# Five matrix places in the convolution, row scatters without pacing waits, and the second layer's output bias added by VectorE

## The reference, cut to what matters

```python
# layer 1, convolution: v, x1, x2 are three projections of the normalised input
y = v
for i, kern in enumerate((k0, k1)):
    y = fft_conv(y, kern) * x[i + 1]          # 128 channels, 128 taps, causal
x = residual + y @ W_out + b_out
# layer 1, experts: 8 experts, each token goes to 2 of them
h = gelu(einsum("td,ndh->tnh", xt, w1) + b1)
out_all = einsum("tnh,nhd->tnd", h, w2) + b2   # b2 is the output bias of the change
out = (take_along_axis(out_all, top_i) * top_w).sum(axis=1)
```

## Time and profile before

| | us |
|---|---|
| median of 3 runs | 1197.08 |
| lowest and highest of them | 1195.99, 1204.09 |
| the profiled execution, its own time | 1201.37 |
| span of its trace, first to last instruction | 1199.5 |
| convolution: first to last gate | 746.4 to 876.0 |
| experts of layer 1: first to last evacuation | 888.5 to 1158.6 |

### The profile page before, as it was taken

How to read it: one execution, slowest core, us unless ns; L and a number is a source line. 1 busy time by engine, 2 the same in 40 slices (tenths; PEclk the granted TensorE clock), 3 DMA queues, 4 the chain that set the end, 5 groups by cost and what they waited for, 6 DMA issues and landing times. The chain is left out here.

```text
span 1199.5 us, 21003 instructions
## 1 busy us (share of the span) xinstructions
PE 1015.5 (85%) x7025; PEld 881.2 (73%) x7025; DVE 946.0 (79%) x1636; ACT 543.9 (45%) x1511; POOL 788.7 (66%) x685
## 2 busy tenths in 40 slices
PE   5636777798999999999834699988989999999994
PEld 4612333367888888888724599988889999999994
DVE  7777999999999999999999874111268887778848
ACT  1301111157888787888714583000045555555541
POOL 4147766658888888888878357777636665656640
PEclk9868777899999999999956989999999999999998
DMA  9923233325565565665372033999912222442239
GB/s 290 377 83 133 91 127 126 116 69 157 172 189 168 173 175 171 178 185 173 93 293 106 36 102 102 322 292 378 347 51 66 70 68 65 124 148 68 66 116 343
DMA packets 119884, 192.20 MB, mean 160 GB/s; under 512 B 16426, under 2 KB 88190, under 8 KB 117730
## 3 DMA queue, kind: packets, MB, share of 16 engines
q1 hardware_dynamic: 100896, 154.30, 40.4%
q0 software_dynamic: 17408, 35.32, 8.0%
q10 hardware_dynamic: 1474, 1.24, 0.4%
HBM read 123.77 MB, written 67.03 MB: 159 GB/s over the span
## 5 line engine op out<-in xcount | busy, mean ns | idle before, releaser
L560 POOL DMA_INDIRECT y_tok<-FF,yidx x278 | 306.2, 1102 | 164.6 <-DVE FF L1440 103.3
L552 POOL DMA_INDIRECT sorted_x<-XN,idx x256 | 247.7, 967 | 99.1 <-issue 79.1
L887 PE MATMUL ps<-FF 128*128 128x128 f32 x1680 | 204.7, 275 | 0.0
L887 PEld LDWEIGHTS ps<-FF 128*128 128x128 f32 x1680 | 195.8, 192 | 12.0 <-issue 9.0
L344 POOL TENSOR_TENSOR BG<-TPB 128x2048 f32<-128x2048 f32 (+1 forms) x42 | 160.9, 3858 | 14.1 <-DVE BG L1268 13.7
L918 PE MATMUL ps<-BG,cst 128*128 128x512 f32 x176 | 106.8, 775 | 47.9 <-DVE BG L1242 47.9
L1277 DVE TENSOR_TENSOR BG<-ps,TPB 128x1024 f32<-128x1024 f32 x128 | 147.3, 1212 | 0.0
L1286 DVE TENSOR_REDUCE BG<-BG 128x256 f32<-128x4096 f32 x32 | 139.4, 4358 | 0.0
L869 PE MATMUL ps<-FF 128*128 128x256 f32 x568 | 134.5, 380 | 0.0
L918 PEld LDWEIGHTS ps<-BG,cst 128*128 128x128 f32 x176 | 43.2, 252 | 106.3 <-issue 55.3
L631 ACT ACTIVATE FF<-ps,FF 128x256 f32<-128x256 f32 x284 | 114.9, 479 | 7.3 <-PE ps L869 7.0
(11 more groups left out here) (229 smaller groups left out, 2106.2 us busy)
## 6 DMA issues: line engine op xcount, KB each, us to landing
FF<-in_moe SPq DMA_DIRECT2D x71, 514.0 KB
TPB<-in_kpad SPq DMA_DIRECT2D x22, 1024.0 KB, 8.0
sorted_x<-TPB SPq DMA_DIRECT2D x36, 520.0 KB, 4.3
FF<-sorted_x SPq DMA_DIRECT2D x135, 130.0 KB, 2.2
BG<-y_tok SPq DMA_DIRECT2D x12, 1024.0 KB, 9.9
FF<-in_kpad SPq DMA_DIRECT2D x10, 1024.0 KB, 8.0
y_tok<-FF,yidx POOLq DMA_INDIRECT x278
xt_d<-BG SPq DMA_DIRECT2D x16, 256.0 KB, 4.0
```

Source lines behind the costliest of these rows:

```text
L552: pool.indirect_dma_start(sorted_x[layer], bass.IndirectOffsetOnAxis(ap=idx[:, k, j:j + 1], axis=0), XN[:, j, :], None).then_inc(s_sc[part ...
L560: pool.indirect_dma_start(y_d[layer], bass.IndirectOffsetOnAxis(ap=yidx[:, G % 4, r:r + 1], axis=0), ys[:, G % 4, r * D:(r + 1) * D], None ...
L887: t = pe.matmul(psY[:, r * P:(r + 1) * P], hT[:, G % 2, m, r * P:(r + 1) * P], (wc[:, G % 4, :] if layer == 0 else block_weights(f, r))[:, ...
```

## The change

Four things are changed at once.
- The convolution has five matrix places instead of three. The two new ones lie in `FF[:, 0:4096]`, where the first weight places `wb` are; so the first two `tile_weights`, which stood between the last convolution steps, now follow the convolution.
- `beside_tensor_engine` leaves out its waits in layer 1.
- The output bias is no longer copied per block nor written by a matmul. A resident float32 set `box`, spread to all partitions by one DMA, is read by VectorE: `expert_evac` loads the block's expert number, adds `box[e]` to `psY` into a scratch tile `yb`, waits for that with the new semaphore `s_yb`, and scales from `yb` to `ys`.
- The loops of layer 1 are written in another order: PE does hidden(f), rows_X(f+1), expert_out(f-1); VectorE does rows_T(f+1), expert_evac(f-1), tile_weights(f+3). Four of the 16 copies of the convolution's result stand ahead of the loop, the other 12 in every second tile from the first.

```diff
+TPS = 5
-                    wait(sp, s_cmm, N - 2)
+                    wait(sp, s_cmm, N - TPS + 1)
-                    if cv == 1 and 2 <= n < 2 + E:
-                        expert_weights(n - 2)
+                    if cv == 1 and 5 <= n < 5 + E:
+                        expert_weights(n - 5)
...
-                elif n < 34:
-                    if n >= 6 and n % 4 == 2:
-                        pool.wait_ge(s_pps, min(14 + n // 2, NT // 2))
-                elif n >= 40 and n % 6 == 4:
-                    pool.wait_ge(s_cmm, min((n - 40) // 3 + 1, 2 * D // 8))
...
-                pe.matmul(psY[:, 0:FT].rearrange("p (r d) -> p r d", r=FR), ones3[:, :],
-                          bo[:, G % 4, None, :].to_broadcast([P, FR, D]) if layer == 0 else block_biases(f),
-                          start=True, stop=False)
+                if layer == 0:
+                    pe.matmul(psY[:, 0:FT].rearrange("p (r d) -> p r d", r=FR), ones3[:, :],
+                              bo[:, G % 4, None, :].to_broadcast([P, FR, D]), start=True, stop=False)
...
             for f in range(NF1):
+                hidden(1, f)
                 if f + 1 < NF1:
                     rows_X(1, f + 1)
-                hidden(1, f)
...
-                    t = dve.tensor_copy(block_biases(f)[:, r:r + 1, :], box[:, ds(e, 1), :])
...
                 for r in range(FR):
-                    t = dve.tensor_scalar(ys[:, G % 4, r * D:(r + 1) * D], psY[:, r * D:(r + 1) * D],
+                    e = dve.value_load(eid[0:1, 2 * f + r:2 * f + r + 1], min_val=0, max_val=E - 1)
+                    t = dve.tensor_tensor(yb[:, r * D:(r + 1) * D].rearrange("p (a n) -> p a n", a=1),
+                                          psY[:, r * D:(r + 1) * D].rearrange("p (a n) -> p a n", a=1),
+                                          box[:, ds(e, 1), :], ALU.add)
+                t.then_inc(s_yb, 1)
+                dve.wait_ge(s_yb, f + 1)
+                for r in range(FR):
+                    t = dve.tensor_scalar(ys[:, G % 4, r * D:(r + 1) * D], yb[:, r * D:(r + 1) * D],
                                           xs[:, G % 4, r, D + 1:D + 2], None, ALU.mult)
                 t.then_inc(s_yev, 1)
...
+            gather_outputs(0)
+            gather_outputs(1)
+            gather_outputs(2)
+            gather_outputs(3)
+            rows_T(0)
             tile_weights(2)
-            gather_outputs(0)
-            rows_T(0)
-            rows_T(1)
             for f in range(NF1):
+                if f + 1 < NF1:
+                    rows_T(f + 1)
                 if f > 0:
                     expert_evac(f - 1)
-                if f + 2 < NF1:
-                    rows_T(f + 2)
```

More of the change, by code:

```diff
@@ L102, in mixed_layers @@
         w1s = sb("w1s", [P, W_END])
+        bix = sb("bix", [P, E, MK])
         w3s = sb("w3s", [LAT, LAT + 2 * D + P - LAT + 1])
@@ L171, in mixed_layers @@
         wb = [a[:, i * 1028:(i + 1) * 1028] for a in (FF, TPB) for i in range(4)]
-        box = xg[:, 0, :].bitcast(bf16).rearrange("p (e n) -> p e n", e=E)
-        bix = xg[:, 1, 0:E * MK].rearrange("p (e m) -> p e m", e=E)
-        bot = xg[:, 1, 2 * E * MK:2 * E * MK + 256].bitcast(bf16).rearrange("p (s n) -> p s n", s=4)
+        box = xg.rearrange("p s (e n) -> p (s e) n", n=D)
+        yb = bo[:, :, :].rearrange("p s n -> p (s n)").bitcast(fp32)
         wc = FF[:, 0:4112].rearrange("p (s n) -> p s n", s=4)
@@ L194, in mixed_layers @@
         patr = pat.rearrange("p (r d) -> p r d", r=FILL)
-        tp = [a.rearrange("p (c n) -> p c n", c=8) for a in (TPB[:, 0:2048], TPB[:, 2048:4096], FF[:, 5664:7712])]
+        tp = [a.rearrange("p (c n) -> p c n", c=8) for a in (TPB[:, 0:2048], TPB[:, 2048:4096], FF[:, 5664:7712],
+                                                    FF[:, 0:2048], FF[:, 2048:4096])]
         ps = [ctx.enter_context(nc.psum_tensor(f"ps{i}", [P, 512], fp32)) for i in range(8)]
@@ L281, in mixed_layers @@
         s_gev = sem("second_gate_ready")
-        s_tp = [sem(f"toeplitz_loaded{i}") for i in range(3)]
+        s_tp = [sem(f"toeplitz_loaded{i}") for i in range(TPS)]
         s_cmm = sem("conv_psum")
@@ L888, in expert_out @@
                                       (wc[:, G % 4, :] if layer == 0 else block_weights(f, r))[:, HID + m * D:HID + (m + 1) * D],
-                                      start=False, stop=(r == FR - 1 and m == MK - 1))
+                                      start=(layer == 1 and m == 0),
+                                      stop=(m == MK - 1 and (layer == 1 or r == FR - 1)))
                 t.then_inc(s_Y, 1)
@@ L1019, in convolution @@
                         c0 = k * NT + NT // 2
-                        pe.matmul(bank[:, k * NT:k * NT + n0], tp[N % 3][:, k, diag:diag + P], V[:, col:col + n0],
+                        pe.matmul(bank[:, k * NT:k * NT + n0], tp[N % TPS][:, k, diag:diag + P], V[:, col:col + n0],
                                   start=True, stop=False)
-                        t = pe.matmul(bank[:, c0:c0 + n1], tp[N % 3][:, k, P - diag:2 * P - diag], V[:, col:col + n1],
+                        t = pe.matmul(bank[:, c0:c0 + n1], tp[N % TPS][:, k, P - diag:2 * P - diag], V[:, col:col + n1],
                                       start=False, stop=True)
@@ L1394, in _ @@
             dve.wait_ge(s_resst, 16 * 8)
-            dve.memset(xg[:, :, :], 0.0).then_inc(s_bz, 1)
             for g in range(NG):
@@ L1420, in _ @@
                 conv_gate(1, n, X2)
-                if n == 12:
-                    dve.wait_ge(s_bx, 32)
-                    dve.wait_ge(s_wx, 16 * E)
-                if n in (12, 14):
-                    tile_weights((n - 12) // 2)
             dve.wait_ge(s_cev, 32)
+            dve.wait_ge(s_bx, 32)
+            dve.wait_ge(s_wx, 16 * E)
+            tile_weights(0)
+            tile_weights(1)
             def rows_T(f):
@@ L1459, in _ @@
                     tile_weights(f + 3)
-                if 0 < f < 2 * NG and f % 2 == 0:
-                    gather_outputs(f // 2)
+                if f % 2 == 0 and f // 2 + 4 < NG:
+                    gather_outputs(f // 2 + 4)
                 if f >= NF1 - 18 and f % 2 == 0 and f < NF1 - 2:
```

14 lines of the change are left out of this document (5 added, 9 removed).

## The result

The kernel after takes 1246.9 us (median of 4 runs, 1243.48 to 1248.06) against 1197.78 (4 runs, 1195.99 to 1204.09): the ratio is 1.041 with a 95% interval of 1.038 to 1.043. Its profiled execution took 1247.55 us, span 1245.7, so it stands 0.7 above the median where that of before (1201.37) stands 3.6 above, or 4.3 above the median of three runs that the prediction had.

What follows compares the result with a forecast made beforehand. PE was taken to bound the experts before, the psY ring after. Terms -9 + 40.8 + 13 + 1.8 = +46.6 us on the profiled 1201.4 gave 1248; less 4.3 for the median, 1244 rounded; range 1212 to 1264.

Steps and rivals of the forecast that it cites:

- front, to the first index copy: Convolution and start of the experts: five places and unpaced scatters start the experts 9 us earlier (bounds 0 and 12).
- 67 plain steps: Experts of layer 1: 67 tile steps at 4.63 us each, 310.2 us against 269.4, 40.8 us more.
- extra copies: Expert tiles with a convolution-result copy (12) or residual add (8) come late: 13 us together, bounds 0 and 17.
- from the last index copy to the end: Last evacuation, on the path to the end, grows from 0.68 to 2.44 us: 1.8 us more.
- The ring with two exposed loads: Experts: output and evacuation alternate through one bank psY; two number loads lengthen this to 4.63 us, above PE's 3.79.
- A waiting instruction holds up the loads behind it: VectorE's evacuation: number loads behind the index copy that waits for psY cannot start until it does; 0.76 us each.
- The rival that they run ahead of it: Evacuation: both loads finish while the index copy waits for psY, PE stays the bound, 1177 us; chance 0.08.
- The price of a load: VectorE's evacuation: a number load delays the next instruction needing it by some 0.76 us, bounds 0.73 and 0.80.
- The new order costs nothing by itself: Expert loop: PE's hidden products ahead of the transposes add nothing at 4.63 us per tile, with 0.25 to spare.
- The bias matmul's 0.11: Experts: without the bias matmul PE loses 0.11 us per tile, its own work becoming 3.79 us.
- The rival of one hidden load: Evacuation: first load hides under the transposed-rows copy, VectorE's list binds at 4.15, 278 us; total 1216 or 1207; chance 0.07.
- The clock: PE in the experts: granted clock stays 1.00; the rival that it falls gave 1280 us, chance 0.06.

Runs made afterwards that it cites:

- e1: Kernel after, with the bias adds reading fixed rows of the bias set, so the evacuation's two number loads are gone; 1201.44 us, ratio 1.0025.
- e7: Kernel after, with expert numbers kept in registers from the weight copies instead of loaded again, and the expert loop in the old order; 1190.11 us, ratio 0.994.

## Why the prediction was right, and where not

The median was forecast at 1244 us, in a range of 1212 to 1264, and came to 1246.9; against the median of before that is 49.1 us more. Against the span of before (+46.2 measured, +46.6 predicted) the four terms are:

| term | predicted | measured |
|---|---|---|
| front, to the first index copy | -9 | -4.9 |
| 67 plain steps | +40.8 | 67 x 4.51 - 269.4 = +32.8 |
| extra copies | +13 | 317.4 - 302.2 = +15.2 |
| from the last index copy to the end | +1.8 | 44.7 - 41.6 = +3.1 |

The sum is closer than its parts: -8.0 and +7.6 cancel, and that it came out within half a microsecond is luck. One part was also added up wrongly: 6 and 8 us of extra copies make 14, not 13.

- **The ring with two exposed loads** was the right mechanism: without the loads 45 us go, with the loads ahead of the wait 42, with two banks the plain tile falls, with a shorter list it doesn't. Its size was 4.52 and not 4.63. The loads were right (0.73 and 0.76 against 0.76 each); the two scalings out of SBUF take 0.48, where I took the 0.60 of those out of PSUM and had named 0.5 as the other bound.
- **A waiting instruction holds up the loads behind it**: shown, by the loads ahead of the wait. The rival that they run ahead of it has fallen for a waiting index copy; where the copy has no wait, the first load does run early (987.6). The Trainium skill ("Advanced Engine Details and Errata", Sequencer Loop) lets one expect the other; this kernel's rows disagree with it wherever the instruction ahead waits.
- **The price of a load**: the Trainium skill ("DMA: Bandwidth & Descriptors", Latency and other measured facts) has about 600 ns; the two of the ring measured 0.73 and 0.76. The third, right behind another load, is near the 600.
- **The new order costs nothing by itself** was wrong. It costs 7.5 us with the loads (317.4 to 309.9) and 7.1 without (272.2 to 265.1). I checked one tile, found 0.25 us to spare and put the late tiles down to VectorE's extra work alone; the loop goes over two tiles, has 2 x (4.51 - 4.39) to spare, and what the extra copies exceed that by is lost. In the old order the pairs hide in the ring (9.02). So half of what the extra copies cost belongs to the order. PE's waits show it too: the one for the scaling, forecast on each tile, is there 20 times, while ahead of the hidden products PE stood 41 times and 26.9 us in all, where I had nothing.
- **The bias matmul's 0.11** for each tile is real: plain 3.79 in e1 and e7.
- **The rival of one hidden load** gave 278 us plus the copies for VectorE's list; the one-load kernel measured 295.2, near the 296 that these make, but set by the two-tile loop, which the rival hadn't in it either; the fit is chance.
- **The front** missed by 4 us, 2.6 of them in one step. The last gate came as said (863), but the last scatter at 868.63 and not at 866; from there to the first transposes it took 4.8 us, the 4.7 of the earlier trace rows. I had given back all 5.1 us of the scatters' waits. In the kernel before a scatter waited 2.18 us for PE at 848.54 and the next 3.15 without a releaser; now there is one wait of 4.92 at 849.93, also without one. A paced scatter that is let go earlier reaches the same stall earlier. What stalls it is open. The high DMA share of these stretches (1.06 in the earlier trace rows) doesn't explain it alone: in every trace the stall stands ahead of the 114th of the 128 scatters, and the first layer has one ahead of its 114th too, where the share is 0.52 before and 0.54 after (225 to 231 us).
- **The clock** stayed at 1.00 in the experts up to 1160 us, as said; from 1165 to 1201 us it is 0.96.

## What to carry to other kernels

Before a register load is placed, ask what stands ahead of it: behind an instruction that waits for another engine it costs all of its 0.7 us, behind work that doesn't wait and lasts as long almost nothing, and a number that was loaded once can stay in its register. When a ring is costed, write down the other loops too, those over two tiles among them: here the ring, the two-tile loop and PE lay at 4.51, 4.39 and 3.79 us, and breaking the first alone gave nothing. An edit that comes bundled with others (here the new order) is worth a run by itself: the version with the bias add, without its loads and without the new order is the only one here that beats the kernel before by more than 0.2%, and it does so by 0.6%.

## What was not expected of the hardware

- Two loads hoisted ahead of a wait cost 0.09 us for each plain tile (3.88 against 3.79), against 0.72 in the ring.
- GpSimd's scatters stop once between 842 and 853 us without a releaser in every kernel, ahead of the 114th: 3.15 us in the kernel before, 4.92 after, 4.79 with five places and paced scatters, 4.60 with three places and free ones. The 114th scatters of the two layers in the kernel before:

```profile
230.90 0.95 POOL L552 DMA_INDIRECT sorted_x<-XN,idx  x1 [4.01 <-issue]
...
852.67 0.96 POOL L552 DMA_INDIRECT sorted_x<-XN,idx  x1 [3.15 <-issue]
```

- Loads that follow one another directly don't overlap: the third added 0.6 us, of which the TENSOR_LOAD itself is 0.3.
